# One Mamba-2 layer and a ternary feed-forward layer on one core: another order at the start, dt of batch 1 earlier, a tile's last product and the first two products by halves

## The reference, cut to what matters

```
h  = rmsnorm(x, ln1_w)
z, xs, Bs, Cs, dt = split(h @ w_in.T)            # 512, 128, 128, 512 and 4 columns
xs, Bs, Cs = silu(causal_conv(xs | Bs | Cs, 4 taps) + conv_b)
dt = softplus(dt + dt_bias);  a = -exp(A_log) * dt
# per chunk of 128 tokens, per head (4 heads):
cs = cumsum(a)
Yd = ((C @ B.T) * exp(cs_q - cs_k) * lower_triangle) @ (X * dt)
S  = exp(cs_end) * S + (exp(cs_end - cs) * B).T @ (X * dt)     # carried from chunk to chunk
Y  = Yd + exp(cs) * (C @ S_before) + D * X
h1 = x + (Y * silu(z)) @ w_out.T
h2 = h1 + (silu(rmsnorm(h1, ln2_w) @ gate_w.T) * (.. @ up_w.T)) @ down_w.T
x1 = layernorm(x + h2)
q(w) = round(clip(w / (mean|w| + eps), -1, 1)) * mean|w|        # ternary weights
out = layernorm(x1 + ((x1 @ q(w_gate).T) * (x1 @ q(w_up).T)) @ q(w_down).T)
```

## Time and profile before

| | |
|---|---|
| median of 3 runs | 478.28 us (476.49 to 478.68) |
| the profiled execution | 479.27 us |
| its span (first to last instruction) | 477.4 us |
| PE busy | 97% of the span |
| DVE, ACT, POOL busy | 71%, 54%, 49% |
| DMA | 40.81 MB, mean 85 GB/s |

### The profile page before, as it was taken

How to read it: one execution, slowest core, us unless ns; L and a number is a source line. 1 busy time by engine, 2 the same in 40 slices (tenths; PEclk the granted TensorE clock), 3 DMA queues, 4 the chain that set the end, 5 groups by cost and what they waited for, 6 DMA issues and landing times.

```text
span 477.4 us, 6373 instructions
## 1 busy us (share of the span) xinstructions
PE 462.0 (97%) x2068; PEld 370.6 (78%) x2068; DVE 336.8 (71%) x581; ACT 259.6 (54%) x508; POOL 232.7 (49%) x283
## 2 busy tenths in 40 slices
PE   7998979999999989999999999999999999999995
PEld 7886757776777768888878888888887777788883
DVE  3674465774677797766798899984968665587274
ACT  4889647868657666557333334322618765658000
POOL 5483555435673398776887400017028455652022
PEclk9999989999999999999999999999999999999999
DMA  8720212112232305435323326620110010000022
GB/s 241 246 89 1 89 44 67 45 44 89 89 90 88 133 0 199 141 125 168 120 89 132 125 92 223 212 98 1 44 45 0 1 45 23 1 1 1 0 89 88
DMA packets 14432, 40.81 MB, mean 85 GB/s; under 512 B 2368, under 2 KB 2368, under 8 KB 14400
## 3 DMA queue, kind: packets, MB, share of 16 engines
q1 hardware_dynamic: 14400, 40.41, 25.2%
HBM read 38.30 MB, written 2.10 MB: 85 GB/s over the span
## 4 chain that ended last, share of the span: by engine, by line
PE 83%; DVE 7%; ACT 6%; issue 3%; POOL 2%; POOLq 0%; DVEq 0%; ACTq 0%
PE psA L1723 6%; PE psA L1725 6%; PE psA L1738 6%; PE psA L1740 5%; PE psA L1731 3%; PE psA L1729 3%; PE psB L1934 3%; PE psB L1930 3%; PE psB L1933 3%; PE psB L1740 2%; PE psB L1738 2%; PE psB L2033 2%; PE psB L2021 2%; PE psB L2032 2%; PE psB L2022 2%
## 5 line engine op out<-in xcount | busy, mean ns | idle before, releaser
L799 POOL TENSOR_SCALAR var<-mv 128x1 f32<-128x1 f32 x16 | 4.5, 280 | 107.7 <-DVE mv L1299 107.6
L861 POOL TENSOR_TENSOR beta<-wsum,beta 128x512 fp32r<-128x512 f32 x28 | 36.2, 1313 | 20.9 <-ACT beta L1066 20.9
L1188 ACT ACTIVATE c<-c 128x512 f32<-128x512 f32 x14 | 8.9, 632 | 47.4 <-DVE c L1525 47.4
L1711 PE MATMUL psA<-xT_h,win_h 128*128 128x512 f32 x80 | 32.1, 401 | 0.0
L1712 PE MATMUL psA<-xT_l,win_h 128*128 128x512 f32 x80 | 31.2, 391 | 0.0
L1425 DVE SCALAR_TENSOR_TENSOR xbc<-psA,convw_sb,xbc 128x511 f32<-128x511 f32 (+2 forms) x36 | 26.9, 747 | 4.3 <-ACT xbc L1125 3.4
L1198 ACT ACTIVATE act_hl<-act 128x512 fp32r<-128x512 f32 x28 | 17.0, 627 | 18.5 <-PE psB L1934 12.2
L990 POOL TENSOR_TENSOR int_l<-int,int_h 128x512 fp32r<-128x512 f32 x11 | 14.3, 1296 | 17.9 <-ACT int_h L1269 17.9
L1723 PE MATMUL psA<-xT_h,beta 128*128 128x512 f32 x56 | 22.0, 393 | 1.0 <-DVE tT_l L1346 0.7
L1575 DVE TENSOR_TENSOR act_hl<-act,act_hl 128x512 fp32r<-128x512 f32 x28 | 19.0, 686 | 3.9 <-ACT act_hl L1198 3.9
L1725 PE MATMUL psA<-xT_l,beta 128*128 128x512 f32 x56 | 21.8, 389 | 0.0
(11 more groups left out here) (337 smaller groups left out, 1603.3 us busy)
## 6 DMA issues: line engine op xcount, KB each, us to landing
raw<-in_f_gu_t SPq DMA_DIRECT2D x22, 512.0 KB, 3.4
raw<-in_w_gu_t SPq DMA_DIRECT2D x14, 512.0 KB, 3.7
raw<-in_f_dn_t SPq DMA_DIRECT2D x10, 512.0 KB, 3.3
raw<-in_w_gu_t SPq DMA_DIRECT2D x14, 256.0 KB, 2.7
raw<-in_w_dn_t SPq DMA_DIRECT2D x7, 512.0 KB, 3.3
raw<-in_w_in_t SPq DMA_DIRECT2D x5, 512.0 KB, 4.0
x<-in_hidden SPq DMA_DIRECT2D x8, 256.0 KB, 4.9
out<-x SPq DMA_DIRECT2D x8, 256.0 KB, 2.0
```

Of the source, the lines that this page charges most:

```text
L861: nc.gpsimd.tensor_tensor(beta[:, f % 2, 1, cols], wsum[:, f % 2, cols], beta[:, f % 2, 0, cols].bitcast(F32), ALU.subtract).then_inc(gb_l ...
L1711: nc.tensor.matmul(ps, sh, mh, start=i == 0, stop=False)
```

## The change

- The weights of the first norm (`ln1_w`) come from the host as 128 equal rows and are loaded as a plain tile, behind all four tiles of x and not between tiles 1 and 2. Load 0 is issued right behind, ahead of the six small constants.
- `load` 0 (ACT's `win_h`) stands ahead of the turned tiles. Products 0 and 1 of batch 0 are cut by halves of tokens: `halfhigh` (high·high) and `halflow` (high·low) for tokens 0 to 255 once tiles 0 and 1 are turned, beside tiles 2 and 3; the step `inproj` then does tokens 256 to 511, and the weights' low part over all 512. `low1` is DVE's `win_l` of load 0. `dt` 0 follows product 1. `prepare` comes later, and its `diag_d` (POOL) is the step `diagonal`.
- `WARM_UP` 24 instead of 30; `KEEP_WARM` 4 and 2 behind tiles 1 and 2, none behind tile 3.
- `dt` 1 moves from behind product 9 of batch 0 to ahead of (`chunk`, 0, 0); `dtturn` 1 and `dtlog` 1 move from behind (`chunk`, 0, 1) to behind product 9. `dtend` 1 stays. In product 0 of batch 1 the four high·high matmuls come ahead of the waits for `xT_l`.
- At the end of batch 1's scan, `tlow` 3 comes ahead of `tlast` 2, and POOL's sum of x (`xsum` 1, 3) two products later. The waits count accordingly.
- The last `ffndown1` is two jobs of 22 matmuls of 256 columns in two banks; `ffnsum`, the last scaling and the last store go by halves of 256 features too.

```diff
-    steps += [("turn1", 0), ("turn1", 1), ("prepare",), ("turn1", 2), ("turn1", 3), load("in", 0)]
-    steps += [("dt", 0), load("in", 1), load("in", 2)]
+
+
+    steps += [load("in", 0), ("turn1", 0), ("turn1", 1), ("turn1", 2), ("halfhigh", 0), ("turn1", 3), ("halfhigh", 1),
+              ("halflow", 0), ("halflow", 1), ("low1",)]
+    steps += [load("in", 1), ("prepare",), load("in", 2)]
...
+        if j == 1:
+            steps.append(("dt", 0))
...
+        if j == NX + NZ - 2:
+            steps.append(("dt", 1))
         if j == NX + NZ - 1:
-            steps.append(("dt", 1))
+            steps += [("dtturn", 1), ("dtlog", 1)]
...
-            steps += [("dtturn", 1), ("dtlog", 1), ("dtend", 1)]
+            steps.append(("dtend", 1))
...
-            steps += first + [("gsplit", 0, 0)] + before + after + held[:1] + thigh + held[1:] + [("tlow", *turned)]
-            steps += second + [("p1", NPRE - 1), ("gsplit", 0, 1)]
+            steps += first + [("gsplit", 0, 0)] + after + held[:1] + thigh + [("tlow", *turned)] + held[1:]
+            steps += second + [("p1", NPRE - 1), ("gsplit", 0, 1)] + before
...
-WARM_UP = 30
-KEEP_WARM = {1: 11, 2: 8, 3: 9}
+WARM_UP = 24
+KEEP_WARM = {1: 4, 2: 2}
...
+        elif kind == "halfhigh":
+            a.append(("in", 0, *at))
+        elif kind == "inproj" and at not in ([0, 0], [0, 1], (0, 0), (0, 1)):
...
-            load_x(0)
-            load_x(1)
-            sp.dma_start(ln1_sb[:], ln1_w.to_broadcast([P, D])).then_inc(ln1_loaded, 16)
-            for t in range(2, NC):
+            for t in range(NC):
                 load_x(t)
 
-            sp.dma_start(wdt_raw[:], w_dt).then_inc(consts_loaded, 16)
-            sp.dma_start(alog_sb[:], a_log.to_broadcast([P, H])).then_inc(consts_loaded, 16)
-            sp.dma_start(dtb_sb[:], dt_bias.to_broadcast([P, H])).then_inc(consts_loaded, 16)
-            sp.dma_start(dskip_sb[:], d_skip.to_broadcast([P, H])).then_inc(consts_loaded, 16)
-            sp.dma_start(convw_sb[:], conv_w).then_inc(consts_loaded, 16)
-            sp.dma_start(convb_sb[:], conv_b).then_inc(consts_loaded, 16)
+            sp.dma_start(ln1_sb[:], ln1_w).then_inc(ln1_loaded, 16)
...
+                if n == 0:
+                    sp.dma_start(wdt_raw[:], w_dt).then_inc(consts_loaded, 16)
+                    sp.dma_start(convw_sb[:], conv_w).then_inc(consts_loaded, 16)
+                    sp.dma_start(convb_sb[:], conv_b).then_inc(consts_loaded, 16)
+                    sp.dma_start(alog_sb[:], a_log.to_broadcast([P, H])).then_inc(consts_loaded, 16)
+                    sp.dma_start(dtb_sb[:], dt_bias.to_broadcast([P, H])).then_inc(consts_loaded, 16)
+                    sp.dma_start(dskip_sb[:], d_skip.to_broadcast([P, H])).then_inc(consts_loaded, 16)
...
-            for t in range(NT):
+            for t in range(NT - 1):
                 sp.wait_ge(out_ready, t + 1)
                 sp.dma_start(out[t], x[:, t, :]).then_inc(out_stored, 16)
-            sp.wait_ge(out_stored, 16 * NT)
+            for i, cols in enumerate(halves_of_tile):
+                sp.wait_ge(out_ready, NT + i)
+                sp.dma_start(out[NT - 1, :, cols], x[:, NT - 1, cols]).then_inc(out_stored, 16)
+            sp.wait_ge(out_stored, 16 * (NT + 1))
...
-                        v.wait_ge(t_low, 2 * c)
+                        v.wait_ge(t_low, 2 * c + (c == NC - 1))
...
+                elif step == ("ffnsum", 1, NC - 1):
+                    t = tile_of(step)
+                    v.wait_ge(ln1_ready, t + 1)
+                    for i, cols in enumerate(halves_of_tile):
+                        job = ("ffndown", 1, at[1] + i)
+                        v.wait_ge(*done_b(job))
+                        nc.vector.scalar_tensor_tensor(out=x[:, t, cols], in0=bank_b(job)[:, cols],
+                                                       scalar=scl[:, 13:14], in1=x[:, t, cols], op0=ALU.mult,
+                                                       op1=ALU.add).then_inc(half_summed, 1)
+                        v.wait_ge(half_summed, i + 1)
+                        v.wait_ge(bn_ready, NT + t)
+                        link(nc.vector.bn_stats(bn6[:, i, :], x[:, t, cols]))
+                    nc.vector.bn_aggr(mv[:, NT + t, :], bn6[:]).then_inc(bn_ready, 1)
...
+                    for cols in halves_of_tile if t == NT - 1 else [slice(0, D)]:
+                        nc.vector.tensor_scalar(x[:, t, cols], x[:, t, cols], mv[:, NT + t, 0:1], rstd[:, i:i + 1],
+                                                ALU.subtract, ALU.mult).then_inc(out_ready, 1)
...
-            def split_product(ps, parts, low_weights):
+            def split_product(ps, parts, low_weights, low_moving=()):
 
 
                 for i, (sh, _, mh, ml) in enumerate(parts):
                     nc.tensor.matmul(ps, sh, mh, start=i == 0, stop=False)
+                    if not low_moving:
+                        nc.tensor.matmul(ps, sh, ml, start=False, stop=False)
+                for turned in low_moving:
+                    pe.wait_ge(*freed_b(turned))
+                for sh, _, _, ml in parts if low_moving else ():
                     nc.tensor.matmul(ps, sh, ml, start=False, stop=False)
                 if low_weights:
...
+                elif kind == "halfhigh":
+                    j = at[0]
+                    if j == 0:
+                        pe.wait_ge(xTh_ready, TURNS.index(("turn1", 1)) + 1)
+                        pe.wait_ge(in_high_ready, 1)
+                    ps = open_a(("in", 0, j))
+                    for k in range(KD):
+                        nc.tensor.matmul(ps[:, 0:L // 2], win_h[:, 0, of_input(j, k)], xT_h[:, k, 0:L // 2],
+                                         start=k == 0, stop=False)
+                elif kind == "halflow":
+                    j = at[0]
+                    for c in range(2):
+                        pe.wait_ge(*freed_b(("turn1", c)))
+                    for k in range(KD):
+                        nc.tensor.matmul(bank_a(("in", 0, j))[:, 0:L // 2], win_h[:, 0, of_input(j, k)],
+                                         xT_l[:, k, 0:L // 2], start=False, stop=False)
+                elif step in (("inproj", 0, 0), ("inproj", 0, 1)):
+
+                    j = at[1]
+                    ps = bank_a(("in", 0, j))
+                    pe.wait_ge(xTh_ready, TURNS.index(("turn1", NC - 1)) + 1)
+                    for k in range(KD):
+                        nc.tensor.matmul(ps[:, L // 2:L], win_h[:, 0, of_input(j, k)], xT_h[:, k, L // 2:L],
+                                         start=False, stop=False)
+                    for c in range(2, NC):
+                        pe.wait_ge(*freed_b(("turn1", c)))
+                    for k in range(KD):
+                        nc.tensor.matmul(ps[:, L // 2:L], win_h[:, 0, of_input(j, k)], xT_l[:, k, L // 2:L],
+                                         start=False, stop=False)
+                    pe.wait_ge(*in_split(0))
+                    for k in range(KD):
+                        done = nc.tensor.matmul(ps, win_l[:, 0, of_input(j, k)], seq(xT_h, k, 0), start=False,
+                                                stop=k == KD - 1)
+                    done.then_inc(a_done, 1)
...
-                    pe.wait_ge(t_low, 2 * NC - 1)
+                    pe.wait_ge(t_low, 2 * NC - 2)
...
+                elif step == ("ffndown1", NC - 1):
+
+                    c = at[0]
+                    for i, cols in enumerate(halves_of_tile):
+                        ps = open_b(("ffndown", 1, c + i))
+                        for f in range(FF):
+                            high, low = int_parts(1, f)
+                            nc.tensor.matmul(ps[:, cols], high[:, chunk(c)], q_dn[:, f, cols], start=f == 0,
+                                             stop=False)
+                            done = nc.tensor.matmul(ps[:, cols], low[:, chunk(c)], q_dn[:, f, cols], start=False,
+                                                    stop=f == FF - 1)
+                        done.then_inc(b_done, 1)
...
-        "ln1_w": a["ln1_w"].reshape(1, D),
+        "ln1_w": np.broadcast_to(a["ln1_w"].reshape(1, D), (P, D)),```

**The start of PE's queue.** PE's first rows, before. `ident` into psA are the turns whose results are not read, `xn` the normed tiles.

```order
L1763 MATMUL psB<-ident,xn 128x128 [waits nrm_ready]
L1763 MATMUL psB<-ident,xn 128x128 x3
L1775 MATMUL psA<-ident 128x128 x8
L1763 MATMUL psB<-ident,xn 128x128 [waits nrm_ready]
L1763 MATMUL psB<-ident,xn 128x128 x3
L1775 MATMUL psA<-ident 128x128 x9
L1801 MATMUL psA<-xT_h,wdt 128x512 [waits wdt_ready,xTh_ready]
L1801 MATMUL psA<-xT_h,wdt 128x512 x3
L1806 MATMUL psA<-xT_l,wdt 128x512 [waits b_free2,b_free3,b_free1,b_free0]
L1806 MATMUL psA<-xT_l,wdt 128x512 x3
L1711 MATMUL psA<-xT_h,win_h 128x512 [waits b_free3,b_free2,in_high_ready,b_free1,b_free0]
L1712 MATMUL psA<-xT_l,win_h 128x512
```

31 lines of the change are left out of this document (19 added, 12 removed).

## The result

The changed kernel takes 473.89 us, median of 6 (473.63 to 475.16), beside 478.48 us for the kernel before (476.29 to 479.96): ratio 0.992, 95% interval 0.989 to 0.995. It is faster, as forecast, but by 4.6 us where 9.3 were forecast, and 0.9 us above the range of 466.5 to 473.0. Between the two profiled executions the gain is 5.4 us (479.27 to 473.88), and 5.6 between their spans.

What follows compares the result with a forecast made beforehand. PE, busy 97% of the span, was taken to bound the kernel. Terms 2.7 + 4.7 + 1.5 + 0.4 = 9.3 us off the median 478.28 gave 469.0 us, range 466.5 to 473.0.

Steps and rivals of the forecast that it cites:

- Term 1: Start up to `dtturn` 1: reordered loads, half products and `dt` 1 filling a gap gain 2.7 us (bounds 1.0 to 3.5).
- So ACT's queue moves 2.1 to 2.2 us: Start: load 3 lands at 17.8, ACT takes it 2.7 us earlier, less 0.6 for `dt` 0's copy.
- Term 2: Batch 1's scan: `outproj` 0,0 loses its 3.1 us wait and the lower clock, gaining 4.7 us (bounds 0 to 5.0).
- DVE's dt operations by 50.9, the copy of S (ready 51.7) by 52.5: Scan, DVE times in us: the copy frees the bank of chunk 1's `seg`, needed about 53.3, with 0.8 us slack.
- Term 3: End of batch 1's scan: shorter waits at `p6` 0 and `p7` 0 gain 1.5 of 1.6 us (bounds 0.5 to 1.9).
- The needed operation now comes ahead of two others: End of batch 1's scan: earlier `tlow` helps the waits of 0.9 and 0.7 us at `p6` 0 and `p7` 0.
- At nothing: ... `xsum` 1,3: Moving POOL's sum of x at the end of batch 1's scan was counted as worth nothing.
- Term 4: Tail: halves save 0.6 us of DVE behind the last matmul and cost 0.2, gaining 0.4 (bounds 0 to 0.6).
- Half matmuls don't show their weight loads: Rival, start and tail: 256-column matmuls do show them; 474.7 us at 0.188 each (chance 0.05), 483.3 if serial (0.04).
- the start gives nothing back through the clock: Rival, start: with fewer idle turns the clock rises late, 1.8 to 2.2 us lost, 471.2; chance 0.14.
- the stall moves: Rival, scan: dt's operations wait for ACT's exp, delaying `seg`; up to all of Term 2 lost, 473.7 us; chance 0.15.
- `p6` 0 and `p7` 0 lose under 0.3 together: Sign for the end of batch 1's scan: PE's two waits there together stay under 0.3 us.

Runs made afterwards that it cites:

- e3: Changed kernel with load 2 (weights of products 4 and 5) issued ahead of tiles 4 to 7 of x: 472.78 us, ratio 0.989.
- e7: Changed kernel with the third edit taken back and load 2 issued ahead of tiles 4 to 7: 472.32 us, ratio 0.988.
- e2: Changed kernel with the third edit taken back: 472.69 us, ratio 0.989.
- e10: Changed kernel with the norm's weights loaded between tiles 1 and 2 as before: 473.58 us, ratio 0.988.
- e8: Changed kernel with the last turned tile of batch 1 moved behind `dtend` 0, ahead of product 7: 473.36 us, ratio 0.988.
- e1: Kernel before with only the dt move (`dt` 1 ahead of chunk 0, `dtturn` 1 and `dtlog` 1 behind product 9): 473.20 us, ratio 0.990.
- c0: Changed kernel run once more, nothing edited: 473.58 us, ratio 0.991.
- e9: Changed kernel with the third edit taken back, load 2 ahead of tiles 4 to 7, and the last turned tile early: 472.03 us, ratio 0.985.
- e5: Changed kernel with only POOL's sum of x (`xsum` 1,3) back at its old place, `tlow` 3 still first: 473.62 us, ratio 0.990.
- e11: The kernel of e5 run again: 472.86 us, ratio 0.987.
- e6: Kernel before with the start edits alone (load order, halves of products 0 and 1, fewer idle turns, later `diag_d`): 478.15 us, ratio 0.999.
- third edit: Part of the change: `tlow` 3 ahead of `tlast` 2, and `xsum` 1,3 two products later; the changed kernel without it took 472.69 us.

## Why the prediction was right in its sign and wrong in its size

- **Term 1, the start: 2.7 forecast, 1.4 measured.** The half products began at 10.52 (forecast 10.4), the stall for `win_l` was 0.16 (forecast 0.45), and product 2 started at 18.96 (forecast 18.55; 2.2 gained instead of 2.6). The step that failed is "So ACT's queue moves 2.1 to 2.2 us", which rested on load 3. It moved 1.04: the last tile's `xT_h` starts at 41.85, 42.89 before, where the forecast had it end at 41.3. ACT stood still earlier, 2.6 us for load 2 (which it had without a wait before), which SP issues at 8.98, behind six constants, load 1 and tiles 4 to 7, each an issue of 0.43 to 0.62 us. e3 moved it and won 0.8 (0.4 in e7 beside e2); e10 moved something else and won nothing. A smaller part was that `dt` 1 waits for a tile that stands far back on ACT (e8). Against e1, which has the old start, the start edits are worth some 0.5 at `dtturn` 1 (48.81 in c0 beside 49.31), a difference as small as the scatter of the landings; the six profiles with the changed kernel's start all have `dt` 1 earlier than e1's 42.73, though.
- **Term 2, dt 1 out of the scan: 4.7 forecast, 5.0 measured.** The mechanism was right: no wait, clock 1.00. Its 1.6 for the clock holds beside the profiled execution; the third of the executions before that have no drop lose only the wait. `outproj` 0,0 started near 59.0 and not 57.5, without harm. e1 shows that the edit does it alone. That it met no new wait was in part luck. "DVE's dt operations by 50.9, the copy of S (ready 51.7) by 52.5" was 2 to 3 us off: they end at 53.7 and 54.45, since ACT's exp came at 51.6 and three of the small operations were stretched to 0.7 to 1.1 us. `seg`, wanted at 53.3 by my reckoning, starts at 54.67, 0.2 behind the copy, because the start had brought PE less lead than forecast. With more lead it became a wait (e8, e9).
- **Term 3, `tlow` ahead of `tlast`: 1.5 forecast, -0.95 measured.** Two steps failed. "The needed operation now comes ahead of two others": the second wait grew by just what the first lost (e5, e11), a case that I named and set aside. And "At nothing: ... `xsum` 1,3": moving it costs the 0.95 (e2 beside e5 and e11).
- **Term 4, the tail: 0.4 forecast, 0.1 measured.** "The last scaling and store by halves are worth nothing" is wrong by 0.2, and PE's loss is 0.3, not 0.2.
- **The rivals.** Half matmuls don't show their weight loads: they stand 0.12 apart, with load records of 0.19. The Trainium skill (TensorE: Matmul & The Clock Gate, Part 3, "What overlaps and what doesn't") says that a weight load overlaps a running matmul only if it goes to another row group; these rows speak against it, since the loads take the whole array. That the start gives nothing back through the clock falls too (1.00 from 10 to 19). That the stall moves was false for the changed kernel, by 0.2 us, and true for the next step, e8. Of the signs set down, `dt` 1 "near 41.3" (42.49) and "`p6` 0 and `p7` 0 lose under 0.3 together" (1.7) failed.

The best version, e9, takes back the third edit, puts load 2 first and turns the last tile early: 472.03, ratio 0.985 (0.982 to 0.988). On its chip it is 1.5 us below e10, which times as the changed kernel did. Against the kernel before on that chip it is 7.7 by medians, but 9 of those 11 executions have the drop of the clock; beside the two without it (476.68 and 476.81) it is 4.7.

Still open: how much of the start's gain is real in the time (e6 leaves 0 to 1 us), and what decides whether the clock falls behind a wait and for how long. The kernel before shows all three cases. Its executions at 476.3 to 477.0 have granted clocks of 0.998 and 0.999, so no drop like that of its profile (0.995 as a whole), though none of them was profiled; that they had the 3.1 us wait all the same is likely, not shown.

## What to carry to other kernels

When a start is moved, follow the chain of the engine that comes next back to the DMA issues: the first transfer that lands late sets that engine's whole queue, and a small constant costs an issue like a large tile. An order that serves one reader first moves the wait to the next reader, if the work ahead of both is the same; and two short waits were better here than one long one: the clock fell behind none of those of 0.6 to 0.9 us, and sometimes behind one of 1.8. When the times of a kernel fall in groups, look at each execution's granted clock before a gain is read from medians. An operation on POOL moved "into idle time" must be checked against what DVE does beside it, not only against its own reader.

## What the runs showed of the hardware

- The same kernel, with the same wait of 1.8 us, ran on at 2.4 GHz in one execution and at 1.2 GHz for 3.4 us in another (granted clock 1.00 and 0.53). Eight profiles have a wait of 1.7 to 1.8 us at `p7` 0, and a drop followed it in one of them; the wait of 3.1 us was followed by one in both profiles that have it (the kernel before and e6). Of 39 executions of the kernel before, 13 have a mean granted clock of 0.998 or 0.999, 13 of 0.993 to 0.995 and 13 of 0.989 or 0.990, and their median times are 476.8, 478.9 and 480.1 us.
- 256-column matmuls with full weight loads stand 0.120 us apart, where half of the 0.2265 of 512 columns would be 0.113.
- DVE operations without PSUM input that lie beside POOL's take 1.2 us for 0.37 (128x256), and tiny ones (128x16) 0.7 to 1.1 for 0.17.
